# Four graph layers on one core: one of ScalarE's two evictions of layer 0's hidden features moves from the head of a step to the end of the step before

## The reference, cut to what matters

```
A_hat = (adj + I) scaled by 1/sqrt(degree) on both sides
agg = einsum('nm,bmd->bnd', A_hat, x)
h   = relu(batchnorm(agg @ W1.T + b1))        # W1: 256 x 128, so two halves of 128 hidden features
out = batchnorm(h @ W2.T + b2)
```

## Time and profile before

| what | value |
|---|---|
| median of 3 runs | 1078.5 us (1076.91 to 1078.81) |
| the profiled execution | 1076.58 us, of which the span of the trace is 1074.5 |
| busy share of the span | PE 85%, DVE 61%, ACT 54%, POOL 17% |
| granted PE clock, mean | 0.878 |
| evictions L1003 | 32, from 52.9 to 149.6 us |
| PE's L473 waiting for an eviction L1003 | 15 times, 17.1 us |

### The profile page before, as it was taken

One profiled execution on the slowest core, in us unless ns is written; L12 is line 12 of the kernel. 1 busy time (PEld: TensorE's weight loads), 2 busy tenths in 40 slices (PEclk: granted clock), 3 DMA queues, 4 the chain that ended last, 5 costly groups with the idle time before them and its releaser, 6 DMA issues.

```text
span 1074.5 us, 13132 instructions
## 1 busy us (share of the span) xinstructions
PE 911.8 (85%) x3841; PEld 604.0 (56%) x3841; DVE 652.8 (61%) x2203; ACT 579.0 (54%) x1480; POOL 186.6 (17%) x470
## 2 busy tenths in 40 slices
PE   4688776868767675599999999999999998999995
PEld 3455444445445554476788777786444465654443
DVE  4667775655667887357535698534544465554676
ACT  0555544745635665257644255535965555664556
POOL 0233333412333333000000000000011121110055
PEclk9799975976855655599999999999999999999998
DMA  9100000000000000000000000000000000000014
GB/s 259 35 2 1 1 1 1 0 1 1 1 1 1 1 1 0 1 1 1 1 2 1 1 1 1 2 1 1 1 1 1 1 0 1 1 1 1 0 40 117
DMA packets 14328, 12.97 MB, mean 12 GB/s; under 512 B 897, under 2 KB 11057, under 8 KB 14257
## 3 DMA queue, kind: packets, MB, share of 16 engines
q1 hardware_dynamic: 14018, 11.98, 4.1%
q10 hardware_dynamic: 238, 0.16, 0.1%
HBM read 7.89 MB, written 4.19 MB: 11 GB/s over the span
## 4 chain that ended last, share of the span: by engine, by line
PE 71%; DVE 17%; ACT 6%; issue 3%; POOL 1%; ACTq 0%; DVEq 0%; DMA 0%; POOLq 0%
PE bank L884 15%; PE bank L908 9%; PE bank L805 3%; PE bank L740 3%; PE bank L750 3%; PE bank L764 3%; PE bank L795 3%; PE bank L473 3%; PE bank L576 2%; PE bank L575 2%; PE bank L704 2%; PE bank L715 1%; PE bank L871 1%; PE bank L813 1%; PE bank L863 1%
## 5 line engine op out<-in xcount | busy, mean ns | idle before, releaser
L1335 ACT ACTIVATE hid_t<-bank,gate_b 128x512 f32<-128x512 f32 (+1 forms) x252 | 150.8, 632 | 67.6 <-PE bank L908 66.5
L908 PE MATMUL bank<-ms,w_t 128*128 128x512 f32 (+1 forms) x288 | 112.9, 536 | 6.9 <-DVE ms L2069 6.9
L1439 POOL COPY hid_t<-feat_t 128x1008 f32<-128x1008 f32 (+1 forms) x12 | 27.9, 2323 | 499.2 <-DVE feat_t L2065 499.2
L884 PE MATMUL bank<-hid_t,w_t 128*128 128x336 f32 (+1 forms) x296 | 106.3, 506 | 1.2 <-DVE x L2073 1.2
L884 PE MATMUL bank<-feat_t,w_t 128*128 128x512 f32 x208 | 93.1, 603 | 0.0
L908 PEld LDWEIGHTS bank<-ms,w_t 128*128 128x128 f32 x288 | 54.6, 193 | 56.7 <-issue 34.4
L884 PEld LDWEIGHTS bank<-hid_t,w_t 128*128 128x128 f32 x296 | 55.9, 190 | 46.0 <-issue 26.1
L1342 ACT ACTIVATE hid_t<-hid_t 128x512 f32<-128x512 f32 (+1 forms) x72 | 41.8, 581 | 52.6 <-DVE hid_t L2051 27.6
L1130 ACT ACTIVATE con<-bank,con 128x1 f32<-128x1 f32 x62 | 16.2, 261 | 99.2 <-PE bank L576 98.8
L884 PEld LDWEIGHTS bank<-feat_t,w_t 128*128 128x128 f32 x208 | 39.1, 189 | 51.0 <-issue 46.7
L575 PE MATMUL bank<-u_t,src_st 128*128 128x127 f32 (+61 forms) x124 | 33.3, 360 | 36.8 <-DVE u_t L1706 36.8
(11 more groups left out here) (425 smaller groups left out, 2090.5 us busy)
## 6 DMA issues: line engine op xcount, KB each, us to landing
out<-x SPq DMA_DIRECT2D x16, 256.0 KB, 3.0
con<-in_constants SPq DMA_DIRECT2D x1, 449.0 KB, 3.3
hid_t<-in_L_gnn_W SPq DMA_DIRECT2D x2, 128.0 KB, 3.6
e_int<-in_L_gnn_src ACTq DMA_DIRECT2D x1, 128.0 KB
l_w<-in_L_gnn_W SPq DMA_DIRECT2D x2, 64.0 KB
wg<-in_L_gnn_Wg SPq DMA_DIRECT2D x2, 64.0 KB
adj_n<-in_adj SPq DMA_DIRECT2D x1, 64.0 KB, 3.2
hid_t<-in_L_gnn_W_lin SPq DMA_DIRECT2D x1, 64.0 KB, 3.3
```

Source lines behind the costliest of these rows:

```text
L884: return mm(bank[4 * u + BANK_OF[g]][:, 0:w], w_t[:, WB_IH + 4 * (it.p - 1) + g, :], lstm_x(n), start=True, stop=(it.k == 0))
L908: mm(bank[4 * u + BANK_OF[g]][:, 0:w], w_t[:, WB_HH + 4 * (it.p - 1) + g, :], lstm_h_of(it.chain)[:, 0:w], start=False, stop=True).then_in ...
L1335: f(dst[:, 0:w], bank[4 * u + BANK_OF[g]][:, 0:w], ACT.Tanh if g == G_G else ACT.Sigmoid, bias=gate_b[:, 4 * (it.p - 1) + g:4 * (it.p - 1) ...
```

## The change

`A_SAVE1` goes from 3 to 2, and the eviction of bank 7 leaves ACT's `beside`. A new function `behind_step` issues it, called at the end of each of the first four steps of a turn. So for each of the 16 tiles the instruction moves from the head of step t+3 to the end of step t+2. It is the same instruction, 16 times, and nothing is added or taken away on any engine.

```
-A_AGG, A_COPY, A_HID0, A_HID1, A_SAVE0, A_SAVE1, A_STATS = 0, 1, 1, 2, 2, 3, 4
+A_AGG, A_COPY, A_HID0, A_HID1, A_SAVE0, A_SAVE1, A_STATS = 0, 1, 1, 2, 2, 2, 4
@@ ACT, beside(slot)
-                if 0 <= slot - A_SAVE1 < TILES:
-                    l0_hidden(slot - A_SAVE1, 1)
                 if 0 <= slot - A_SAVE0 < TILES:
                     l0_hidden(slot - A_SAVE0, 0)
@@ ACT
+            def behind_step(slot):
+
+                if slot is not None and 0 <= slot - A_SAVE1 < TILES:
+                    l0_hidden(slot - A_SAVE1, 1)
@@ ACT, jacobi_turn(i)
                 act_step(h0)
+                behind_step(h0)
                 act_off(i)
                 act_dif(i)
...
                 if h1 is not None:
                     act_vector(h1 + 1)
+                behind_step(h1)
                 act_row(h2)
                 beside(h2)
                 act_step(h2)
                 act_y(i)
+                behind_step(h2)
                 act_row(h3)
                 act_y2(i)
                 beside(h3)
                 act_step(h3)
                 act_vt(i, 0)
+                behind_step(h3)
```

## The result

The changed kernel takes 1071.8 us (median of 5 runs, 1070.91 to 1073.32) against 1078.5 before; the ratio is 0.9944, with an interval of 0.9929 to 0.9958. So it is 6.7 us faster, where 9.2 us were forecast.

The account below looks back on a forecast made before the run. PE's own order, with the chain making the rank update's vector, was taken as the bound; three turns' 7.6 + 1.0 + 0.77 - 0.1 gave 9.3, rounded to 9.2 us, so 1078.5 became 1069.3 us, range 1061 to 1075.5.

Parts of the forecast that it names:

- h1: Second step of a Jacobi turn: the copy of A waits for DVE's L1721, so the gain is only 0.45 us.
- h2: Third step of a turn: L527 waits for Jacobi's factors, so 0.45 us is carried through and nothing added.
- h0: First step of a turn: PE's queue alone holds the rank update L575, so removing its wait gains 1.04 us.
- h3: Fourth step of a turn: PE's 1.20 us wait goes, but DVE's vector then limits L575; 1.04 us of its own.
- ACT's price at h1: Moved eviction in ACT's queue at h1: at most 0.15 us left uncovered, 0.1 taken as reaching DVE's chain.
- 0.57 - 0.19 - 0.23: Eviction's cost at h1 less ACT's idle time before L1139 and before L1083, leaving 0.15 us at most.
- ACT's price at h0 and h3: Moved eviction's 0.57 us fits in ACT's idle time before the row copy, 0.69 and 0.84 us: cost nothing.
- Step 17: Late first-stage step: L1132 already starts 0.04 us behind L1721, so nothing gained and 0.1 us delay remains.
- that of the clock: Rival, 8 in 100: later stages' clock turns out differently; six second-stage steps falling low lose 9.4 us, 1078.7, or the reverse.
- the partial one: Rival, 15 in 100: the rank update's vector comes later than read, another wait takes most; about 4.5 us gain, 1074.
- the PE-only one: Rival, 7 in 100: PE is the only bound, so all 17.1 us of waits come back, 1061.4 us.
- the slower one: Rival, 4 in 100: ACT's row copy is late by its full 0.57 us in 15 steps, 8.6 us lost, 1087.

Follow-up runs that it names:

- e8: Changed kernel plus one unneeded 512-column product ahead of L527 in h2 of the first stage, filling PE's pause; 1065.41 us, ratio 0.9895.
- e9: e4 plus the same unneeded 512-column product in the pause of h2; 1074.93 us, 0.9978 of the kernel before.
- e3: Changed kernel, but eviction moved only at the ends of h2 and h3, left at the head of the next step elsewhere; 1070.53 us, 0.9929.
- e4: Changed kernel, but eviction moved only at the end of h0, left at the head of the next step elsewhere; 1087.99 us, 1.0091.
- e5: Changed kernel with ACT's new order, but PE's second-half product again waits for the same step's eviction of bank 4; 1086.74 us, 1.0080.
- e6: Changed kernel with the moved eviction issued twice, the first time into a tile not yet in use; 1084.46 us, 1.0056.
- e10: Changed kernel with the eviction in the same step, but behind the aggregation's copy and ahead of the column L1133; 1070.71 us, 0.9934.
- e7: Changed kernel with PE's layer 0 products put ahead of Jacobi's transposition L527 in h2 of the first stage; 1071.49 us, 0.9934.
- e11: e10 with PE's layer 0 products also put ahead of L527 in h2, as in e7; 1068.85 us, 0.9907.

## Why the prediction was right, and where its size was off

The time lies in the range, and the sign and the mechanism were right: PE's wait was the price, and the stage without the clock's falls gains 97.40 - 87.68 = 9.7 us (e8), where 9.2 were forecast. That the two agree so well is in part luck, since the terms of h1 and h2 came out by another way than forecast. By steps, taken from rank update to rank update in turn 2:

- h0, forecast 1.04: from the h3 before it to h0's, 24.54 - (111.44 - 93.22) = 6.32 us became 21.78 - (107.41 - 90.79) = 5.16, **1.16**. A likely reason: where PE does not wait, a product starts before the profile's modelled end of the one ahead (L473 at 88.59, and the one ahead of it runs by the profile from 88.27 to 88.76), so the idle time in the rows was a little short of what the wait cost.
- h1 and h2, forecast 0.45 together: 104.72 - 93.22 = 11.50 became 101.63 - 90.79 = 10.84, **0.66**. The limit by L1728 was there, but the split between the two steps was wrong. L527, which waits for DVE's factors, stands 102.10 - 93.22 = 8.88 us behind h0's rank update before, and 99.66 - 90.79 = 8.87 after: of h1's gain nothing is carried to it, where 0.45 were forecast. The 0.66 comes between L527 and h2's rank update, 2.62 us before and 1.97 after, by h2's own wait of 0.47, which the prediction put at nothing. e9 tells the same: with only h1's wait gone, L527 still stands 100.25 - 91.38 = 8.87 us behind, and the 0.31 us a turn come with h2's wait, 0.15 us instead of 0.47.
- h3, forecast 1.04: 111.44 - 104.72 = 6.72 became 107.41 - 101.63 = 5.78, **0.94**, with the vector as the limit, as described.
- ACT's price at h1, forecast 0.1 and at most 0.15: h1's row copy is **0.35** late (e3, e4, e5). The step that failed is 0.57 - 0.19 - 0.23. The 0.23 us of idle stood behind the row copy, before L1083, and could not cover an instruction ahead of it; only 0.19 could.
- ACT's price at h0 and h3, forecast 0: right at h0, where the cover is then gone (e6, e10). At h3 the row copy still has 0.26 us of idle time ahead of it in the changed kernel, so it is not late by ACT.
- Step 17, forecast -0.1: 5.34 us before (144.0 to 149.3), 5.76 after, so -0.4; steps 16 and 18 won 0.3 and 0.6.

The sum was thus 0.5 us too small, and yet the forecast was 2.5 us too large. The term that was missing is the clock in the first stage itself. I read "granted clock 1.00 here" as a property of the stage, and put the clock's risk only on the later ones, where it turned out to cost nothing (0.3 us). In fact the high level depended there, at least in part, on where PE's idle time lies between its work. With the waits gone, h2 has one pause of 1.33 us instead of 0.60 and 0.47; two falls behind it took 2.7 us back, and filling it gives them back (e8). Of the rivals, that of the clock came true in kind, at another place and a third of its price; the partial one did not, the PE-only one did not (h1 and h3 are limited by DVE), and of the slower one only the late row copies came.

What stays open: which pause brings a fall. The clock falls in turns 1 and 3 of the changed kernel and not in turn 2, which has the same pause; in e3 and e5 it falls behind h1's wait, which the kernel before has at the same length without a fall. The moment may play a part, as the spread of the runs of e7 and e11 suggests; no run here shows it.

## What to carry to other kernels

Where a wait stands before one engine's queue, read what its removal is worth from the instruction on which the chain waits, not from the length of the wait; and count an idle stretch as cover only for instructions behind it. When instructions move, look at PE's granted clock in each stage before counting the gain: here falls took 2.7 of 9.7 us, and in e4 far more than the whole gain, though none of PE's pauses need grow for a fall (e3). A product that no one needs, put into the pause ahead of a fall, is a cheap test for that, and here the two fastest kernels have it.

## What I had not expected of the hardware

The granted clock of a stage that ran at 1.00 throughout fell after a change that made PE busier over the whole stage: 59.0 us of 74 before, 66.7 after, though that stretch holds more steps after, and slow products count as longer busy. The same stretch of the kernel before:

```profile
61.00:135.00 74.00, 59.01 (x300) 37.37 (x299) 51.80 (x183) 42.49 (x142) 25.13 (x80) 1.00 0.00 1
```

and of the changed kernel:

```profile
61.00:135.00 74.00, 66.69 (x326) 42.34 (x325) 55.68 (x200) 45.98 (x154) 27.99 (x88) 0.95 0.01 1
```

The undisturbed turn 2, which holds the same work in both, before and then after, tells the same: PE is busy for 19.5 us of 24.5, and of 21.8.

```profile
89.53:114.07 24.54, 19.54 (x100) 12.40 (x100) 17.54 (x61) 14.11 (x47) 8.24 (x26) 1.00 0.01 1
88.37:110.15 21.78, 19.52 (x100) 12.42 (x101) 17.33 (x61) 14.05 (x48) 8.33 (x26) 1.00 0.01 2
```

In e4 the eviction of one step in four, moved to the end of the step before, made the kernel 1.0091 of before (1088.0 us), with three falls in this stage. The falls stand at the same steps in both profiles of the changed kernel, while early in the program, before step 3, the two profiles of the kernel before differ by 2.3 us through the moment at which the clock rises.
